# A graph network on one core: one of two products per batch of sort columns moves to ScalarE, with two tables of hits, a buffer cleared in chunks, and a sort spread over 140 of 157 steps

## What is computed

```python
agg = jnp.zeros_like(x).at[src].add(edge_attr)               # 100000 rows -> 6250
h   = jnp.concatenate([x, agg, x_with_cond], axis=1)
x   = x + relu(h @ W1.T + b1) @ W2.T + b2
ht  = relu(layernorm_relu(x) @ W1' + b1')
msg = sigmoid(w * ht[src] + b_param)                          # one gathered row per edge
fsum = segment_sum(msg, dst, num_segments=6250)               # 100000 rows -> 6250
c   = (log(s / (1 - s)) - b_param) / w                        # s = clip(fsum)
out = relu(normalised(concat([ht, c]) @ Wn + bn));  result = x + out
```

## Time and profile before

| | |
|---|---|
| median of 3 runs | 2775.89 us (2775.79 to 2778.08) |
| the profiled execution | 2782.92 us, span 2781.2 us |
| PE busy | 1995.4 us (72%), 9329 matmuls |
| DVE (VectorE) busy | 2027.4 us (73%), 6057 |
| ACT (ScalarE) busy | 1334.5 us (48%), 4292 |
| POOL (GpSimd) busy | 1804.1 us (65%), 1687 |
| gathers, L649 | 785 from the table, 778.3 us; 628 from the edges, 635.9 us |

### The profile page before, as it was taken

How to read it: one execution, slowest core, us unless ns; L and a number is a source line. 1 busy time by engine, 2 the same in 40 slices (tenths; PEclk the granted TensorE clock), 3 DMA queues, 4 the chain that set the end, 5 groups by cost and what they waited for, 6 DMA issues and landing times.

```text
span 2781.2 us, 37581 instructions
## 1 busy us (share of the span) xinstructions
PE 1995.4 (72%) x9329; PEld 1382.7 (50%) x9329; DVE 2027.4 (73%) x6057; ACT 1334.5 (48%) x4292; POOL 1804.1 (65%) x1687
## 2 busy tenths in 40 slices
PE   1468895567777877778987567777777777876785
PEld 1356673355355345345665445534534435544474
DVE  2674453877897897898674488789899799753586
ACT  0133333444744744745325544474464574564554
POOL 1476566777777777775012377777777777777336
PEclk9678887788988999998998768899999999886898
DMA  9897767734633333332565533333333333333233
GB/s 383 242 199 154 150 138 176 184 102 113 165 106 103 103 99 99 103 97 78 181 213 200 184 101 101 102 102 99 101 103 99 102 104 97 103 105 106 82 131 115
DMA packets 181579, 370.26 MB, mean 133 GB/s; under 512 B 32281, under 2 KB 100659, under 8 KB 178818
## 3 DMA queue, kind: packets, MB, share of 16 engines
q0 software_dynamic: 93168, 219.39, 31.0%
q1 hardware_dynamic: 77010, 113.58, 12.6%
q10 hardware_dynamic: 11200, 35.00, 3.2%
HBM read 281.48 MB, written 99.46 MB: 137 GB/s over the span
## 4 chain that ended last, share of the span: by engine, by line
DVE 35%; PE 27%; issue 13%; DMA 10%; POOL 7%; SPq 4%; DVEq 2%; ACT 2%; ACTq 0%; POOLq 0%
PE bank L1393 25%; DVE agg L1155 16%; POOL store L649 6%; DMA store<-g_table,idx_all 4%; DVE oh L1087 3%; DVE hits L1083 3%; DVE store L1079 3%; DVE cum L1012 3%; DMA store<-in_edge_attr,idx_all 2%; DVE cum L1042 2%; DVEq L1147 2%; DMA agg_copy<-agg 1%; SPq L451 1%; DVE msk L905 1%; POOL agg_copy L623 1%
## 5 line engine op out<-in xcount | busy, mean ns | idle before, releaser
L1393 PE MATMUL bank<-store,oh 128*128 (+2 forms) x6770 | 1458.8, 362 | 525.8 <-DVE agg L1155 136.4
L1393 PEld LDWEIGHTS bank<-store,oh 128*128 128x128 f32 (+1 forms) x6770 | 946.3, 166 | 1015.2 <-issue 449.8
L1155 DVE TENSOR_TENSOR agg<-bank,agg 128x256 f32 x1845 | 769.0, 417 | 319.0 <-PE bank L1393 239.1
L649 POOL DMA_INDIRECT store<-g_table,idx_all x785 | 778.3, 991 | 254.7 <-issue 168.7
L789 ACT ACTIVATE oh<-dist 128x128 f32<-128x128 f32 x1845 | 534.7, 304 | 825.0 <-PE bank L1393 794.1
L649 POOL DMA_INDIRECT store<-in_edge_attr,idx_all x628 | 635.9, 1013 | 197.0 <-issue 130.4
L781 ACT ACTIVATE dist<-iota,nloc_all 128x128 f32<-128x128 f32 x1845 | 582.6, 386 | 68.6 <-DVE nloc_all L1127 67.9
L623 POOL DMA_INDIRECT agg_copy<-agg x160 | 252.5, 1578 | 197.7 <-ACT agg L744 111.7
L1087 DVE TENSOR_TENSOR oh<-hits,v 125x512 f16<-125x512 f16 x720 | 285.1, 419 | 7.1
L1079 DVE TENSOR_TENSOR store<-iota,ttab 125x628 f16<-125x628 f16 x360 | 172.3, 479 | 144.0 <-PE bank L1393 143.7
L1393 PE MATMUL bank<-agg 128*128 128x256 f32 (+2 forms) x480 | 139.9, 452 | 90.9 <-DVE agg L1176 44.0
(11 more groups left out here) (196 smaller groups left out, 1472.6 us busy)
## 6 DMA issues: line engine op xcount, KB each, us to landing
agg_copy<-store ACTq DMA_DIRECT2D x4, 6400.0 KB, 35.7
agg<-in_edge_attr SPq DMA_DIRECT2D x39, 512.0 KB, 4.6
store<-in_x SPq DMA_DIRECT2D x72, 256.0 KB, 4.4
agg_copy<-agg_copy POOLq DMA_DIRECT2D x16, 800.0 KB, 7.0
store<-g_table,idx_all POOLq DMA_INDIRECT x785
store<-in_edge_attr,idx_all POOLq DMA_INDIRECT x628
pre_scratch<-store SPq DMA_DIRECT2D x25, 256.0 KB, 5.2
agg<-agg_copy SPq DMA_DIRECT2D x25, 256.0 KB, 8.4
```

The source lines that it names most:

```text
L649: gp.indirect_dma_start(out=store[:, at % RING * D:(at % RING + 1) * D], out_offset=None, in_=table_dram, in_offset=bass.IndirectOffsetOnA ...
L1155: dve.tensor_tensor(to, pt[n % TB][:, 0:D], to, ALU.add).wait_op(s_mm, n + 1, "sem-ge").then_inc(s_acc, 1)
L1393: return pe.matmul(o, l, r, start=start, stop=stop, skip_group_check=skip)
```

## The change

ScalarE forms the second product of a batch (`second_product`), four activations, one per column, with `scale2`, an f32 copy of `v2`, as the scale; in sort 0 both products stay on VectorE. So a batch has three atoms (`COLUMN_OPS` 3). `hits` gets two places. The place of `second_product` in ScalarE's program is after the one-hots of the quad `(n + 6) // 4`, n being the number of the job at whose step the hits are made. `s_col` now counts two per batch, and VectorE's own product of a batch waits until both products of the batch before it are there. `LAG` goes from 5 to 4, the atoms end at step 140 and not 146. To make room, `lw1` and `wn` are kept in the sort's `msk` tile and loaded late, `lw1` once sort 4 has ranked its keys (in group 3) and `wn` once sort 8 has (in group 7). The memset of `agg` is cut into 25 chunks, each after its own product.

```diff
-COLUMN_OPS = 4
+COLUMN_OPS = 3
+COLUMN_LEAD = 6
-LAG = 5
-LAST_STEP = 146
+LAG = 4
+LAST_STEP = 140
-        hits = sb("hits", [P, BATCH * P], F16)
+        hits = sb("hits", [P, 2 * BATCH * P], F16)
+        scale2 = sb("scale2", [P, COLS])
...
-            sp.dma_start(lw1[:, :, :], a["lw1"].rearrange("(k p) f -> p k f", p=P)).then_inc(s_w3, 16)
-            sp.dma_start(wn[:, :, :], a["wn"].rearrange("(k p) f -> p k f", p=P)).then_inc(s_w3, 16)
...
+            sp.wait_ge(s_rank, G1 + 1)
+            sp.dma_start(lw1, a["lw1"].rearrange("(k p) f -> p k f", p=P)).then_inc(s_w3, 16)
...
+            sp.wait_ge(s_rank, SORTS)
+            sp.dma_start(wn, a["wn"].rearrange("(k p) f -> p k f", p=P)).then_inc(s_w3, 16)
...
-            gp.wait_ge(s_p1, NW)
-            gp.memset(agg[:, :], 0.0).then_inc(s_z2, 1)
+            for n in range(NW):
+                gp.wait_ge(s_p1, n + 1)
+                gp.memset(agg[:, n * CH:(n + 1) * CH], 0.0).then_inc(s_z2, 1)
...
+            def second_product(sig, batch):
+                at = sig * BATCHES + batch
+                act.wait_ge(s_hit, at + 1)
+                for c in range(BATCH):
+                    a, i = divmod(c, 2)
+                    to, by = (t.rearrange("p (a n i) -> p a n i", a=BATCH // 2, i=2)[:, a, :, i]
+                              for t in (ohr[K, at % 2, 1, :], hits[K, at % 2 * BATCH * P:(at % 2 + 1) * BATCH * P]))
+                    r = act.activation(to, by, ACT.Relu, scale=scale2[K, batch * BATCH + c:batch * BATCH + c + 1])
+                r.then_inc(s_col, 1)
...
+                def due_quad(n):
+                    return min(max((n + COLUMN_LEAD) // QUAD, first), last - 1)
...
                     onehots(q)
+                    for (sig, batch), n in hit_jobs.items():
+                        if due_quad(n) == q:
+                            second_product(sig, batch)
...
+                    if sig:
+                        dve.wait_ge(s_col, 2 * BATCHES * sig)
+                        do(dve.tensor_copy(scale2[K, :], v2[K, cols]))
...
                 elif op == 1:
+                    if at >= 2:
+                        dve.wait_ge(s_col, 2 * (at - 1))
+                    dve.tensor_tensor(grid(hit, P), numbers(P), pairs(rtab, 0)(P), ALU.is_equal).then_inc(s_hit, 1)
+                else:
+                    dve.wait_ge(s_hit, at + 1)
                     if at:
-                        dve.wait_ge(s_col, at)
...
+                        dve.wait_ge(s_col, 2 * at)
+                    for v in range(1 if sig else 2):
+                        dve.tensor_tensor(grid(ohr[K, b, v, :], P), grid(hit, P), pairs((v1, v2)[v], sig * COLS)(P), ALU.mult
+                                          ).then_inc(s_col, 1)
```

More of the change, by code:

```diff
@@ L187, in gnn_program @@
         w2T = sb("w2T", [P, KD * D])
-        lw1 = sb("lw1", [P, KD, D])
-        wn = sb("wn", [P, 2 * KD, D])
         b2bc = sb("b2bc", [P, D])
@@ L285, in gnn_program @@
         key16 = area(ETILES // 2).bitcast(I16).rearrange("p (j b) -> p j b", j=EB)
+        lw1, wn = (msk[:, 2 * CH * c:2 * CH * c + 2 * n * D].bitcast(F32).rearrange("p (k f) -> p k f", f=D) for c, n in ((2, KD), (3, 2 * KD)))
         low = area(P)
@@ L789, in onehots, with stage_onehots @@
                     act.activation(ohv[:, n % OHS, :], distv[:, n % (2 * QUAD), :], ACT.Relu, bias=1.0, scale=-1.0).then_inc(s_oh, 1)
-            def stage_onehots(first, last):
+            def second_product(sig, batch):
[7 more added lines that the diff above has]
+                r.then_inc(s_col, 1)
+            def stage_onehots(stage, first, last):
+                hit_jobs = {(g + 1, (a - RANK_ATOMS) // COLUMN_OPS): NTH[jobs_at(stage, g, t)[-1]]
+                            for g, t in steps(stage) for a in atoms_at(stage, g, t)
+                            if RANK_ATOMS <= a < RANK_ATOMS + COLUMN_OPS * BATCHES and (a - RANK_ATOMS) % COLUMN_OPS == 1}
+                def due_quad(n):
+                    return min(max((n + COLUMN_LEAD) // QUAD, first), last - 1)
                 distances(first)
@@ L859, in _ @@
             act.wait_ge(s_t3, 2 + NW)
-            stage_onehots(JOBS1 // QUAD, -(-len(ORDER) // QUAD))
+            stage_onehots(1, JOBS1 // QUAD, -(-len(ORDER) // QUAD))
             def logs(n):
@@ L1074, in numbers @@
                     return iota2[K, 0:width, :].unsqueeze(1).to_broadcast([KP, BATCH // 2, width, 2])
+                hit = hits[K, b * BATCH * P:(b + 1) * BATCH * P]
                 if op == 0:
@@ L1239, in _ @@
             tiles(0)
-            dve.wait_ge(s_w3, 64)
+            dve.wait_ge(s_w3, 48)
             def fold_in(n):
@@ L1304, in _ @@
                 g_out(CHB - 1)
-            dve.wait_ge(s_z2, 1)
+            dve.wait_ge(s_z2, NW)
             tiles(1)
@@ L1472, in columns @@
                 b = at % 2
-                pe.wait_ge(s_col, at + 1)
+                pe.wait_ge(s_col, 2 * (at + 1))
                 def column(t, a, i):
@@ L1662, in _ @@
                 r.then_inc(s_p2, 1)
-            pe.wait_ge(s_w3, 64)
+            pe.wait_ge(s_w3, 48)
             with pe.Fori(0, CBODIES) as i:
@@ L1710, in _ @@
             pe.wait_ge(s_acc, len(ORDER))
+            pe.wait_ge(s_w3, 64)
             def sums_transpose(n):
```

10 lines of the change are left out of this document (1 added, 9 removed).

## The result

Nine runs of the changed kernel took 2763.05 us in the median (2755.51 to 2771.93), nine of the kernel before beside them 2777.20 us: a ratio of 0.9948 [0.9932, 0.9963], 14.4 us less. A second set of runs gave 0.9961 [0.9947, 0.9976]. The profiled execution took 2766.58 us, its span 2764.8.

What follows compares the result with a forecast made beforehand. GpSimd's own pace, drawn out by VectorE, was taken to bound the groups in both layers. Terms 6.5 + 5.1 + 4.4 + 1.0 = 17 us less, from a 2775.9 us median to 2759; range 2740 to 2788.

Steps and rivals of the forecast that it cites:

- the forecast case: Whole kernel: 17 us less, 2759 us, with a band of 2748 to 2769; chance 0.47.
- the light groups: Groups 0, 4 and 1 keep slack and gain 1.7 us each, 5.1 us in all.
- The stretch of the gathers: Columns: each VectorE f16 operation draws GpSimd's gathers out by 0.043 us; 40 fewer a sort save 1.7 us, 13.8 in 8 sorts.
- The prediction's own sign of being wrong: Named beforehand as showing it wrong: the gathers' stretch does not follow the number of f16 operations.
- The new loop: Columns of a HEADED sort: waits between VectorE, ScalarE and TensorE make 1.45 us a step against 1.22 before.
- I take 204.8: 1.3 us less a group, in the five HEADED groups.: Groups 2, 3, 5, 6, 7: engines' path 203.9 us meets GpSimd's need 204.4; 204.8 taken, 6.5 us less in all.
- The memset, 4.4 us: After the memset: with chunks done earlier, VectorE's 128x50 operation is over in about 0.2 us, not 4.70; 4.4 us less.
- The two weights, 1 us: Prologue: 0.77 MB less to load is some 2 us of transfer; 1 us less taken, bounds 0 and 16.
- SyncE's gate as rival: Prologue: SyncE's queue was the gate, up to 15 us more go, 2744 us; chance 0.15 shared with GpSimd alone.
- Sort 0 ... with the same work: nothing.: Prologue: sort 0's columns start two blocks later and come denser; no effect, bounds -3 and +7 us.
- The slower rival: Columns: ScalarE's loop binds at 0.35 us a product, path 211.2 us, whole kernel 15 us slower, 2791; chance 0.19.

Runs made afterwards that it cites:

- e9: The changed kernel with both products on VectorE and three places for products and one-hots of the moves: 2719.97 us, 0.9796 of the kernel before.
- e7: The changed kernel with ScalarE's product on its own semaphore and three places for hits, products and moves: 2710.84 us, 0.9768 of the kernel before.
- e1: The changed kernel with the second product back on VectorE, on a slow chip: 3017.39 us beside 3030.73 for the kernel before, 0.9950.
- e2: The changed kernel with ScalarE's product counted on its own semaphore, on a slow chip: 3040.77 us beside 3030.73 for the kernel before, 1.0022.
- e8: The kernel before with a third place for products and one-hots of the moves, and the two weights loaded late: 2747.48 us, 0.9891.
- e6: The kernel before with the second product left out in sorts 1 to 8, TensorE using the first instead: 2753.99 us in its one run.
- e4: The kernel before with the two weights loaded late alone, on a slow chip: 3033.16 us beside 3030.73, 1.0006.
- e3: The kernel before with the memset in chunks alone, on a slow chip: 3028.57 us beside 3030.73, 0.9996.

## Why the prediction was right, and where it was not

*The total.* 2759 us was forecast and 2763.05 measured, within the range; the forecast case (faster by some 17 us, 14.4 measured) is the one that came. That is partly luck, since two errors cancel: the light groups gave some 8 us more than their term, and the HEADED groups some 7.5 less.

*The stretch of the gathers, "I take 0.043, the even share".* This term was mis-sized, and its form was wrong. In the change the gathers of a sorted group are busy 1.8 to 5.6 us less in place of 1.7, and groups 0, 1 and 4, with slack elsewhere, gave 5.6, 4.0 and 3.6 us in place of 1.7 each. But with three places the move alone is worth 0.021 us an operation (e9 to e7), and on the slow chips 0.03 (e1 to e2), less than the share that I took. Much of the rest comes with the packing, which moves nothing to ScalarE and which I had put at nothing: 10.7 us in the HEADED groups between e8 and e9 (with LAG 4 and the 140 steps). The prediction's own sign of being wrong, a stretch that does not follow the number of f16 operations, so came true. A few gathers that meet a long row of them carry most of it. How the two effects add up with two places, where the change has them, no run on a chip like the first shows; so the share of the 14.4 us that is the product's move stays open.

By the Trainium skill (SBUF — State Buffer, section SBUF: two separate sides) whichever of VectorE and GpSimd starts first holds the shared ports for its whole instruction, and a VectorE operation with two inputs in SBUF does so only against a GpSimd one that reads SBUF. The f16 operations have two such inputs, and a gather reads its indices from `idx_all`. The gather of 1.57 us, 0.63 us over its neighbour with four f16 operations beside it, fits that in kind; the mean, 0.02 to 0.08 us an operation of 0.42 us, is far below its upper end. That a port is what the gathers wait for no run here shows.

*The new loop, "a quad with three batches takes 6.27 us", 1.45 us a step.* Right: 1.42 to 1.43 us a step, products at 0.29 to 0.31 us paced, ScalarE 91% busy, waits of 0.85 us where 0.7 to 0.8 stood. The head took 71.5 us (72.5 forecast), the way to the columns 25 (29.4 for 28 steps; here for 26 adds), the end 22 (18).

*"I take 204.8: 1.3 us less a group, in the five HEADED groups."* This step failed. Groups 2, 5, 6 and 7 have 206.6, 205.2, 204.6 and 206.4 us, and group 3 with its end is 3.0 us longer: 1 us more in all in place of 6.5 less. GpSimd's own need fell to some 202 to 203 us (e6, e7), and the engines' path took its place: GpSimd's true waits for the ring in groups 2, 3, 5, 6 and 7 grew from some 5 to some 15 us, and are gone in e7, whose loop is deeper. Two sides that meet lose far more to each other than the 0.4 us I gave them.

*The memset, 4.4 us.* Right: 4.70 us became 0.18, and some 4 us of it arrive.

*The two weights, 1 us; SyncE's gate as rival.* Right as far as it can be told: the first gather is 1.3 us earlier in e4 than in e3. The "some 2 us of transfer" behind the term have no row: the change's trace moves 138 GB/s from 250 to 400 us of its prologue, by which 0.79 MB would take nearer 6 (my estimate).

*"Sort 0 ... with the same work: nothing."* Right in number, with two places, and wrong as a reading. I took the prologue for transfers alone ("all transfers share busy engines") and did not ask for VectorE's waits in it. They were in the trace: 100.3 us in 38 pieces at the line that the change touches. The third place wins 27 us there, and the change's order of sort 0 (packing and LAG 4) is then worth 13, which the ring of two had hidden.

*The slower rival, a path over 209 us at 0.35 us a product.* It did not come where GpSimd binds. The Trainium skill's rule (ScalarE: Activation LUTs, section Rules for kernel authors) is to multiply on VectorE, for its speed per element. The price agrees: 0.42 us a batch on VectorE, 1.2 on ScalarE. As advice for this kernel it fails in e7 against e9, 8 us for ScalarE; on a slow chip with the loop two deep, e2 against e1 agrees with it, 23 us the other way.

## What to carry over

Before moving work to an idle engine, follow the ring between the engines: count at which place of each program the buffer is given back and asked for again. If it is the same place, each batch pays the skew of the two engines, everywhere the loop runs, and one more place may be worth more than the move (29 us alone and 55 on top of the change, against some 8 for the move). And ask each stretch for its waits, the prologue too, even where another resource looks full.

## What the runs showed that I had not expected

- The same f16 operations on VectorE draw GpSimd's gathers out to 1.060 us or to 1.014 in the columns, by how they stand to each other. In HEADED groups so packed, moving a product away gives the gathers 0.5 us more in all.
- TensorE's granted clock in the prologue was 0.91 in place of 0.82 where the gaps in its work had closed, with 22% more matmuls in the same 150 us.
- Chips differ by 9% on this kernel (2776 against 3031 and 3065 us). GpSimd's instructions and the gathers' packets take the same time on each, but an add follows its matmuls 2.4 us later in place of 0.5, and a group without a sort takes 222 us in place of 196. The kernel with the own semaphore is 0.3% faster than before on one kind and 0.2% slower on the other.
